# Two stacked cross attentions on one core: the second attention's groups summed in pairs, and the transposes N1a placed ahead of the projection q0

## The reference, cut to what matters

```python
# first attention: 8 heads of 40
query = x @ Wq;  keyt = enc @ Wk;  valt = enc @ Wv        # enc: the first 371 rows of ctx, ca: its last 4
hs = _mha(query, keyt, valt)
ca_q1 = einsum('btc,th->bch', ca, Wq_ca)[:, indices, :]   # 112 queries
ca_hs1 = _mha(ca_q1, x, x)
ca_hs2 = _mha(ca_hs1 @ Wq, ca @ Wk_ca, ca @ Wv_ca)
x1 = (hs + ca_hs2) @ Wout + b_out + x
# second attention: 20 heads of 16
q = x1 @ Wq1;  k = ctx @ Wk1;  v = ctx @ Wv1
out = softmax(q k^T / 4) v @ Wo + bo + x1
```

## Time and profile before

| | us |
|---|---|
| median of 3 runs | 744.45 (744.38 to 744.81) |
| the profiled execution | 745.43 |
| its span, first to last instruction | 743.6 |
| PE busy (matmuls) | 702.2 |
| DVE busy | 470.8 |
| ACT busy | 403.7 |
| POOL busy | 294.8 |
| share of PE in the chain that ended last | 73% |

### The profile page before, as it was taken

The page is one execution under the profiler, slowest core; times in us unless marked ns, Lnnn a source line. Parts: engine busy times, 40 slices in busy tenths (PEclk is TensorE's granted clock), DMA queues, the critical chain, the costliest instruction groups (busy, mean ns, idle before and its releaser), DMA issues.

```text
span 743.6 us, 18194 instructions
## 1 busy us (share of the span) xinstructions
PE 702.2 (94%) x6924; PEld 612.6 (82%) x6924; DVE 470.8 (63%) x1028; ACT 403.7 (54%) x923; POOL 294.8 (40%) x401
## 2 busy tenths in 40 slices
PE   8887999999999999999999999999999999999985
PEld 5576888888888888888888888888888888887763
DVE  2563666757576675757566675757667575757662
ACT  2554555555565555665555555556555555554422
POOL 5485662444334253443326245423525343321200
PEclk9889999999999999999999999999999999999986
DMA  9533453342616244252525334361524425160400
GB/s 326 171 106 91 119 130 81 101 88 76 138 47 142 65 120 97 67 118 59 136 58 137 82 92 93 77 136 47 142 69 115 103 65 122 21 143 19 80 9 9
DMA packets 52387, 72.45 MB, mean 97 GB/s; under 512 B 12128, under 2 KB 44256, under 8 KB 52304
## 3 DMA queue, kind: packets, MB, share of 16 engines
q1 hardware_dynamic: 44832, 60.34, 31.9%
q0 software_dynamic: 6144, 9.25, 6.5%
q10 hardware_dynamic: 1328, 1.71, 0.6%
HBM read 20.60 MB, written 4.26 MB: 33 GB/s over the span
## 4 chain that ended last, share of the span: by engine, by line
PE 73%; ACT 10%; DVE 9%; issue 3%; POOL 1%; ACTq 0%; POOLq 0%
PE bankX L1005 29%; PE bankO L1225 8%; PE bankST L1193 7%; PE bankS L1159 6%; PE bankST L1187 5%; ACT arena L577 4%; ACT arena L595 3%; DVE q1T L829 2%; DVE negmax L773 2%; PE bankX L1118 2%; PE bankX L1125 2%; PE bankX L1087 2%; PE bankS L1156 2%; PE bankX L1071 2%; ACT q1T L666 2%
## 5 line engine op out<-in xcount | busy, mean ns | idle before, releaser
L773 DVE TENSOR_REDUCE negmax<-bankS 112x2 f32<-112x750 f32 (+1 forms) x224 | 208.5, 931 | 57.3 <-PE bankS L1159 33.3
L494 POOL DMA_DIRECT2D k_stack<-stage x192 | 96.2, 509 | 180.3 <-DVE stage L809 153.1
L577 ACT ACTIVATE arena<-bankST 125x1344 f32<-125x1344 f32 x80 | 103.5, 1293 | 33.1 <-PE bankST L1193 33.1
L1225 PE MATMUL bankO<-arena,v 125*32 125x112 f32 (+2 forms) x2688 | 107.8, 265 | 6.1 <-ACT arena L577 4.6
L1225 PEld LDWEIGHTS bankO<-arena,v 125*32 125x32 f32 (+2 forms) x2688 | 81.6, 118 | 28.6 <-issue 13.6
L1159 PE MATMUL bankS<-k_stack,q1T 112*112 112x376 f32 x320 | 87.3, 354 | 3.6 <-DVE negmax L773 3.0
L1005 PE MATMUL bankX<-ctx_hi,WH 128*120 128x376 f32 (+2 forms) x192 | 69.0, 359 | 3.0 <-DVE qn L765 2.2
L457 POOL TENSOR_TENSOR w2bd<-w2s,cst 96x896 fp32r<-96x896 f32 x16 | 29.9, 1870 | 99.7 <-DVE w2s L765 99.7
L1193 PE MATMUL bankST<-q1T,k_stack 112*125 112x224 f32 x480 | 66.0, 274 | 0.0
L1005 PE MATMUL bankX<-WH,ctx_hi 128*125 128x320 f32 x192 | 66.0, 344 | 0.0
L1005 PE MATMUL bankX<-ctx_hi,WL 128*120 128x376 f32 (+2 forms) x192 | 64.1, 334 | 0.0
(11 more groups left out here) (141 smaller groups left out, 1546.1 us busy)
## 6 DMA issues: line engine op xcount, KB each, us to landing
k_stack<-stage SPq DMA_DIRECT2D x96, 176.2 KB
k_stack<-stage SPq DMA_DIRECT2D x192, 70.5 KB, 2.6
k_stack<-stage POOLq DMA_DIRECT2D x192, 47.0 KB, 2.0
ctx_raw<-in_ctxT SPq DMA_DIRECT2D x16, 376.0 KB, 3.4
k_stack<-stage SPq DMA_DIRECT2D x48, 117.5 KB
xp<-in_xpad SPq DMA_DIRECT2D x16, 224.0 KB, 3.4
x_raw<-in_xT SPq DMA_DIRECT2D x16, 168.0 KB, 2.4
out<-x1b SPq DMA_DIRECT2D x16, 140.0 KB, 3.3
```

The costliest lines, as they stand in the source:

```text
L494: pool.dma_start(dst, src).then_inc(k1_stacked_pool[b % 2], 16)
L577: nc.scalar.activation(dst[0:KC], bankST[0:KC, :, 0:GROUP * SQ], ACT.Exp).then_inc(exp_done, 1)
L773: nc.vector.tensor_reduce(negmax[:, n % 2, 2 * pair:2 * pair + 2], bankS[0:SQ, :, 0:keys], axis=AX, op=ALU.max, negate=True).then_inc(max_ ...
L1225: last = nc.tensor.matmul(dst, v, src[0:keys, c, SQ * j:SQ * j + SQ], start=(c == 0), stop=(c == NKC - 1))
```

## The change

Two things are changed. First, the groups of the second attention are attended in episodes: k = 0 and 1 together in slot 5, k = 2 and 3 together in slot 0 of the next iteration, k = 4 alone in slot 1; slots 4 and 6 have no `attend`. Before the matmuls of each group of an episode PE waits for that group's exponentials. One `copy_o` on DVE takes the whole episode (224 columns for a pair), and the semaphores `pv_done` and `o_copied` count episodes. Second, in slot 1 the unit N1a (the four transposes of the sums k = 0 to 3 of batch t-2) moves from phase 3 to phase 2, ahead of q0. The bank of a unit follows from its place, so with the move the units of slots 1 and 2 run in the order q1T_1, V1_2, q1T_2, N1a, q0, K1_0, K1_1, and before it was q1T_1, V1_2, q1T_2, q0, N1a, K1_0, K1_1.

```diff
-    ([("q1T_1", -1), ("V1_2", -1)], [("q1T_2", -1)], [("q0", 1)], [("N1a", -2), ("K1_0", 0)]),
+    ([("q1T_1", -1), ("V1_2", -1)], [("q1T_2", -1)], [("N1a", -2), ("q0", 1)], [("K1_0", 0)]),
...
+EPISODES = [e for b in range(B + 1) for e in
+            ([[(0, b, 0)], [(0, b, 1)]] if b < B else []) +
+            ([[(1, b - 1, 0), (1, b - 1, 1)], [(1, b - 1, 2), (1, b - 1, 3)], [(1, b - 1, 4)]] if b > 0 else [])]
+EPISODE = {g: n for n, e in enumerate(EPISODES) for g in e}
+
+def attended_at(t, i):
+    late = scored_at(t, i, LAG)
+    return EPISODES[EPISODE[late]] if late and EPISODES[EPISODE[late]][-1] == late else None
...
-                    act.wait_ge(pv_done, n - 1)
+                    act.wait_ge(pv_done, EPISODE[GROUPS[n - 2]] + 1)
...
-            def copy_o(g):
-                layer, b, k = g
-                n = NUMBER[g]
-                dve.wait_ge(pv_done, n + 1)
+            def copy_o(groups):
+                layer, b, k = groups[0]
+                dve.wait_ge(pv_done, EPISODE[groups[0]] + 1)
...
-                    at = (2 + n % 2) * SQ
-                    dst, src = o1T[:, k, :], bankO[:, at:at + SQ]
+                    dst, src = o1T[:, k:k + len(groups), :], bankO[:, 2 * SQ:(2 + len(groups)) * SQ]
...
-                    if late:
-                        copy_o(late)
+                    if attended_at(t, i):
+                        copy_o(attended_at(t, i))
...
-                    pe.wait_ge(o_copied, NUMBER[layer, b, k] + 1)
+                    pe.wait_ge(o_copied, EPISODE[layer, b, k] + 1)
...
-            def attend(g, transposed):
-                layer, b, k = g
-                n = NUMBER[g]
-                pe.wait_ge(exp_done, n + 1)
+            def attend(groups, transposed):
+                n = EPISODE[groups[0]]
                 pe.wait_ge(mT_copied, transposed)
                 if n > 0:
                     pe.wait_ge(o_copied, n)
...
+                for g in groups:
+                    layer, b, k = g
+                    pe.wait_ge(exp_done, NUMBER[g] + 1)
...
+                            at = (2 + k % 2) * SQ
...
-                    if late:
-                        attend(late, transposed)
-                        attended = NUMBER[late] + 1
+                    if attended_at(t, i):
+                        attend(attended_at(t, i), transposed)
+                        attended = EPISODE[late] + 1
```

More of the change, by code:

```diff
@@ L630, in unit @@
                     elif i == 0:
-                        act.wait_ge(pv_done, NUMBER[0, b - 1, 1] + 1)
+                        act.wait_ge(pv_done, EPISODE[0, b - 1, 1] + 1)
                     nc.scalar.activation(v0[0:KC, i, :].rearrange("p (h d) -> p h d", h=H0)[:, :, 0:D0],
@@ L638, in unit @@
                     elif i == 0:
-                        act.wait_ge(pv_done, NUMBER[1, b - 2, G1 - 1] + 1)
+                        act.wait_ge(pv_done, EPISODE[1, b - 2, G1 - 1] + 1)
                     nc.scalar.activation(v1[b % 2][0:KC, i, :].rearrange("p (h d) -> p h d", h=H1)[:, :, 0:D1],
@@ L779, in copy_mT @@
                 nc.vector.tensor_copy(mT[:, n % MT_BUFS, :], bank_mT).then_inc(mT_copied, 1)
-            def copy_o(g):
-                layer, b, k = g
-                n = NUMBER[g]
-                dve.wait_ge(pv_done, n + 1)
+            def copy_o(groups):
+                layer, b, k = groups[0]
+                dve.wait_ge(pv_done, EPISODE[groups[0]] + 1)
                 if layer == 0:
-                    dst, src = o0T[:, 2 * k:2 * k + 2, :].rearrange("p c q -> p (c q)"), bankO[:, 0:2 * SQ]
+                    dst, src = o0T[:, 2 * k:2 * k + 2, :], bankO[:, 0:2 * SQ]
                 else:
-                    at = (2 + n % 2) * SQ
-                    dst, src = o1T[:, k, :], bankO[:, at:at + SQ]
+                    dst, src = o1T[:, k:k + len(groups), :], bankO[:, 2 * SQ:(2 + len(groups)) * SQ]
+                dst = dst.rearrange("p c q -> p (c q)")
                 nc.vector.tensor_copy(dst, src).then_inc(o_copied, 1)
@@ L911, in _ @@
                 for i in range(SLOTS):
-                    g, before, late = scored_at(t, i), scored_at(t, i, 1), scored_at(t, i, LAG)
+                    g, before = scored_at(t, i), scored_at(t, i, 1)
                     if g:
@@ L1205, in attend @@
                     pe.wait_ge(o_copied, n)
[L1206 to L1213, removed]
@@ L1214, in attend @@
-                for c, j in at_once:
-                    h = GROUP * k + j
+                for g in groups:
+                    layer, b, k = g
+                    pe.wait_ge(exp_done, NUMBER[g] + 1)
+                    if k == 0:
+                        for i in range(NKC):
+                            pe.wait_ge(bank_drained[bank(f"V{layer}_{i}", b)], drained(f"V{layer}_{i}", b))
+                    src = PT[:, NUMBER[g] % 2]
                     if layer == 0:
-                        keys = KC if c < 2 else KC - NTOK
-                        dst = bankO[64 * (j % 2):64 * (j % 2) + 64, (j // 2) * SQ:(j // 2 + 1) * SQ]
-                        v = v0[0:keys, c, 64 * h:64 * h + 64]
-                    else:
[L1221 to L1226, removed]
+                        at_once = [(c, j) for pair in range(2) for c in range(NKC) for j in (2 * pair, 2 * pair + 1)]
+                    else:
+                        at_once = [(c, j) for c in range(NKC) for j in range(GROUP)]
+                    for c, j in at_once:
+                        h = GROUP * k + j
+                        if layer == 0:
+                            keys = KC if c < 2 else KC - NTOK
+                            at = (j // 2) * SQ
+                            dst = bankO[64 * (j % 2):64 * (j % 2) + 64, at:at + SQ]
+                            v = v0[0:keys, c, 64 * h:64 * h + 64]
+                        else:
+                            keys = KC
+                            at = (2 + k % 2) * SQ
+                            dst = bankO[32 * j:32 * j + 32, at:at + SQ]
+                            v = v1[b % 2][0:keys, c, 32 * h:32 * h + 32]
+                        last = nc.tensor.matmul(dst, v, src[0:keys, c, SQ * j:SQ * j + SQ], start=(c == 0),
+                                                stop=(c == NKC - 1))
```

## The result

| | before | changed |
|---|---|---|
| median, us | 744.41 (743.99 to 744.81, 4 runs) | 754.59 (753.31 to 757.57, 4 runs) |
| profiled execution | 745.43 (span 743.6) | 753.89 (span 752.1) |
| iteration, steady part | 42.60 | 43.20 |

The changed kernel is slower: ratio 1.013, 95% interval 1.0092 to 1.0167. The forecast was slower too, but 748.0 with a range up to 752.0; the loss is 10.2 us at the medians and 8.5 between the two profiled executions, and the forecast's own sum was 3.7.

The account below looks back on a forecast made before the run. PE, busy 94%, was taken to bound the kernel through its order of work. Thirteen iterations at +0.42 (+5.5), iteration 1 -0.4, the end -0.4 and -1.0 gave +3.7 us: 748.0, range 743.6 to 752.0.

Parts of the forecast that it names:

- Part 1: Slot 1, N1a ahead of q0: q0 waits for q1T_2's drain, K1_0 starts later, +0.85 us an iteration.
- the 0.10 for a unit behind transposes: Slot 1: the first matmul of a unit behind transposes costs about 0.10 us more, counted for q0.
- the end of K1_0's wait of 0.16: Slot 1: K1_0's wait of 0.16 us on q0's rounding is gone, counted in the +0.85.
- Part 2, slots 4 and 5: Sums leave slot 4, V0_0 comes 0.75 us earlier, the pair in slot 5 costs 0.57: -0.18 an iteration.
- The pair's own price of 0.57: Slots 5 and 0: 24 more instructions in an episode cost 0.57 us, ends 0.54 and 0.60.
- the 0.06 used throughout: All waits: a wait ends 0.06 us after the instruction that it waits for.
- Part 2, slots 6 and 0: V1_0, bound by q1's rounding, starts 0.51 us earlier; W2's wait is filled by added sums: -0.25 an iteration.
- Iteration 1: Only the pairs act in iteration 1: -0.4 us.
- The end: Iteration 15: N1a's transposes slide under a wait, -0.4 us; merges of iterations 15 and 16: -1.0, bounds 0 and -2.
- the pairs bring nothing: Rival: earlier starts in slots 4 and 6 are lost to waits, 754 us, or more likely 751; chance 0.15.
- q0 does not stand still: Rival: slot 1's move costs next to nothing, 737 or 735 us, milder form 742 to 744; chance 0.13 in all.
- nothing measurable: Rival: part 1 at 0.75, added sums at 0.54, full gain at the end, +0.5, about 745 us; chance 0.17.

Follow-up runs that it names:

- e2: Kernel before with only N1a moved ahead of q0, no pairs: 754.76 us, ratio 1.0147.
- e3: Changed kernel with ACT's copy of q1T_2 taken ahead of the exponentials of group 4: 745.02 us, ratio 1.0006 to the kernel before.
- e9: Changed kernel with group 4's exponentials split in two on ACT, the copy of q1T_2 between them: 748.63 us against 745.77 for the kernel before.
- e10: The changed kernel itself run again, unaltered, beside the kernel before: 757.42 us against 745.77, ratio 1.014.
- e1: Changed kernel with N1a back where it was, so only the pairs: 742.36 us against 744.65 for the kernel before, ratio 0.9978.

## Why the prediction was wrong

The direction, the cause and the places were right; the size was not, 3.7 us for 8.5 (10.2 at the medians). By its own steps:

- **Part 1** (q0 waits for q1T_2, +0.85): right, +0.84 thirteen times, shown by the trace, by e2, and one for one by e3 and e9. The two small terms were right as well: the 0.10 for a unit behind transposes, and the end of K1_0's wait of 0.16.
- **Part 2, slots 4 and 5** (-0.18): -0.12. The pair's own price of 0.57 was exact. The start of V0_0, taken 0.75 earlier, came 0.70 earlier (hn0T started 0.09 later than forecast, 0.15 behind its release and not the 0.06 used throughout).
- **Part 2, slots 6 and 0** (-0.25): -0.14. The step that failed is the one from "So V1_0 starts at 367.13" to "The pair in slot 0 then starts at 370.16": it moves all that follows by the same 0.51. V1_0 did start there, but its weights were loaded only then, and another 0.10 was lost at its first matmul. I had 0.10 for q0 and not here. With slots 4 and 5, 0.17 an iteration, **2.1 us** over the 12 and 0.2 in the 13th.
- **Iteration 1** ("only the pairs: -0.4"): +1.0, a miss of **1.4 us**. The step took iteration 1 as a steady one. Without out1 the copy of p3T stood behind the exponentials, 0.41; the transfers of the keys took 0.77 of wait, of which e10 shows 0.54 to be scatter. Both come with the first pair.
- **The end** ("-0.4" and "taken -1.0, bounds 0 and -2", with +0.4 for iteration 14): +0.55 for -1.0, **1.5 us**. The step that failed is that the merges of iterations 15 and 16 bring 1.0: the one of groups 2 and 3 in iteration 16 bought nothing where its sums went, since the transfer of the maxima was then waited for, and cost 1.3 us where they were added. That alone doesn't decide the stretch: e1 has the same 1.3 and came out 1.2 shorter than before, 115.1 (115.4 in e2, 116.5 in e10). How much of the rest is the pairs' and how much the clock's stays open.
- **The medians**: the profiled execution of before lay 1.0 above its median and that of after 0.7 below its own; **1.7 us** of the 10.2 are this. I had taken the first over to the second unchanged. The misses above, 2.1 + 1.4 + 1.5, less 0.2 at the start, are the 4.8 between 3.7 and 8.5.

The rival "the pairs bring nothing" (751 to 754) came nearest in number (754.59 lies just over it), and yet is refuted: the pairs bring 0.245 an iteration. That it came near is luck: the misses at the start and the end made up the difference. "q0 does not stand still" and "nothing measurable" fall with the 13 waits. The range was too narrow also because it had no term for the scatter of start and end.

The Trainium skill's 81 ns a step (TensorE: Matmul & The Clock Gate, Back-to-back issue gap) would have given an estimated 0.49 for the added 24 instructions; the trace has 0.57. The rule of the Trainium skill that matmuls keep program order (TensorE: Matmul & The Clock Gate, The mechanism) agrees with the trace: the exponentials of group 4 were ready at 336.97 + 1.29 = 338.26, their sums stood behind q0, which started at 339.03, and started at 340.38.

## What to carry to other kernels

Where buffers rotate by position in a hand-written order, moving a unit changes whom its neighbours wait for; before a move, write down for the moved unit and the two behind it who drains what they wait for, and what stands ahead of that drain on its engine. Here the reason was a copy of 0.34 us behind exponentials of 1.29 us on ACT, and swapping those two alone took the kernel back to the time of before (745.02 for 744.65). Read the first and the last iterations by themselves, since the units that are missing there were the cover.

## What the runs showed of the hardware

**A wait can cost 0.10 us beyond itself.** V1_0's first matmul takes 0.41 with a wait ahead of it and 0.31 without, the same shapes, because the load of its weights starts with it and not 0.17 ahead. It is not so for every unit: W2 behind the sums has its load start with its first matmul with the wait of before and without it, and its row lasts 0.81 and 0.82.

**The granted clock and the scatter.** The length of a steady iteration was the same within 0.01 us from run to run, but whole runs of the kernel before went from 742.5 to 750.3 us on one chip: 742.5 to 743.4 where the mean granted clock was 0.983 or more (one exception, 745.06), 744.2 to 745.5 at 0.978 to 0.981, and 748.9 to 750.3 at 0.972 to 0.974. On another chip the order was looser (747.3 at 0.980). Which stretches these are, by windows, before and then after (columns: stretch, its length, busy time of PE, PEld, DVE, ACT and POOL with counts, granted clock, share of DMA, GB/s):

```profile
33.00:76.00 43.00, 34.15 (x249) 29.49 (x248) 20.46 (x39) 23.38 (x58) 29.42 (x26) 0.89 0.35 102
400.00:627.00 227.00, 222.54 (x2295) 198.12 (x2293) 149.35 (x331) 132.09 (x300) 89.83 (x127) 1.00 0.42 99
690.00:744.00 54.00, 40.59 (x418) 31.51 (x416) 26.93 (x59) 17.08 (x26) 2.85 (x6) 0.83 0.15 31
```

```profile
33.00:76.00 43.00, 34.64 (x247) 30.01 (x246) 20.47 (x39) 22.68 (x55) 28.98 (x25) 0.87 0.35 101
400.00:635.00 235.00, 225.93 (x2344) 202.23 (x2346) 153.08 (x330) 134.81 (x305) 92.99 (x131) 1.00 0.42 98
700.00:753.00 53.00, 39.23 (x410) 31.89 (x410) 25.45 (x53) 16.72 (x24) 1.33 (x2) 0.82 0.15 29
```

In the steady part the clock is 1.00, that is 2.4 GHz throughout, also with a gap of 0.95 us on PE in each iteration; in the start and the end, where PE waits more, part of the stretch is at 1.2 GHz. How large that part is differs from run to run, and a difference of under 2 us can be read only from the iterations.
